# Two passes instead of three for the value products of both attentions, with a join of half tiles

## The reference, cut to what matters

```python
# layer 0: 16 heads of 32; layer 1: 32 query heads of 64 in 8 groups, keys and queries rotated
w = softmax(q @ k.T / sqrt(hd) + causal_mask)
z = w @ v
x = x + z_of_all_heads @ Wo.T          # layer 1: @ w_out.T
```

## Time and profile before

| | us |
|---|---|
| median of 3 runs | 1908.64 (1906.13 to 1909.9) |
| the profiled execution | 1907.17 |
| its span | 1905.7 |
| first attention, to the last add into X | 0 to 250.7 |
| second attention, to the last add into X | 929.4 to 1483.0 |
| mean granted clock of TensorE, share of full | 0.986 |

### The profile page before, as it was taken

One profiled execution on the slowest core, in us unless ns is written; L12 is line 12 of the kernel. 1 busy time (PEld: TensorE's weight loads), 2 busy tenths in 40 slices (PEclk: granted clock), 3 DMA queues, 4 the chain that ended last, 5 costly groups with the idle time before them and its releaser, 6 DMA issues. The chain is left out here.

```text
span 1905.7 us, 30804 instructions
## 1 busy us (share of the span) xinstructions
PE 1805.5 (95%) x10161; PEld 1565.8 (82%) x10167; DVE 1113.3 (58%) x2769; ACT 807.4 (42%) x2063; POOL 1010.0 (53%) x965
## 2 busy tenths in 40 slices
PE   7999989999999999999888999999999999999996
PEld 5888858788999999899667888888888888867795
DVE  6676785763333333335766666666666757566345
ACT  3767633222222222221256566666665433543231
POOL 3444341397883957895457456456453203116783
PEclk9999999999999999999999999999999999999998
DMA  3556430236653645554343234233331210012666
GB/s 116 173 155 205 144 138 0 78 145 226 231 199 126 214 144 180 191 153 127 90 112 95 68 92 117 57 89 93 84 78 56 74 50 1 24 50 84 213 214 195
DMA packets 104551, 232.54 MB, mean 122 GB/s; under 512 B 20672, under 2 KB 20928, under 8 KB 101328
## 3 DMA queue, kind: packets, MB, share of 16 engines
q1 hardware_dynamic: 84080, 144.31, 25.0%
q0 software_dynamic: 19744, 85.47, 13.6%
q10 hardware_dynamic: 576, 0.79, 0.2%
HBM read 126.23 MB, written 57.93 MB: 97 GB/s over the span
## 5 line engine op out<-in xcount | busy, mean ns | idle before, releaser
L712 POOL TENSOR_SCALAR a_E<-a_E,a_inv 128x128 f32<-128x128 f32 (+3 forms) x384 | 213.9, 575 | 237.7 <-DVE a_inv L848 237.7
L745 ACT ACTIVATE a_E<-a_E,a_top 128x512 f32<-128x512 f32 (+3 forms) x384 | 211.1, 565 | 6.0 <-DVE a_top L842 5.9
L153 PE MATMUL bank<-f_UH,f_XH 128*128 x596 | 200.5, 336 | 8.4 <-POOL f_UL L165 3.4
L153 PE MATMUL bank<-f_UL,f_XH 128*128 x596 | 193.2, 324 | 0.0
L153 PE MATMUL bank<-f_UH,f_XL 128*128 x596 | 193.2, 324 | 0.0
L842 DVE CUSTOM_DVE_ANT_0 a_E<-a_causal,bank 128x512 f32<-128x512 bf16 (+3 forms) x384 | 163.6, 480 | 43.0 <-PE bank L1023 31.5
L153 PE MATMUL bank<-a_PHL,a_VH 128*128 128x512 f32 (+3 forms) x768 | 181.1, 325 | 0.9 <-issue 0.6
L737 ACT ACTIVATE a_PHL<-bank 128x512 fp32r<-128x512 f32 (+1 forms) x288 | 131.0, 528 | 112.6 <-PE bank L1039 112.5
L1821 ACT ACTIVATE f_HH<-bank 128x256 fp32r<-128x256 f32 x220 | 59.8, 323 | 232.2 <-PE bank L2218 232.1
L165 DVE TENSOR_TENSOR a_PHL<-bank,a_PHL 128x512 fp32r<-128x512 f32 (+1 forms) x288 | 153.2, 585 | 5.1 <-ACT a_PHL L737 4.8
L1876 DVE TENSOR_TENSOR f_gate<-bank,f_gate 128x352 f32<-128x352 f32 x79 | 41.3, 522 | 192.1 <-PE bank L153 192.0
(11 more groups left out here) (407 smaller groups left out, 4864.8 us busy)
## 6 DMA issues: line engine op xcount, KB each, us to landing
f_uraw<-f_up POOLq DMA_DIRECT2D x18, 1408.0 KB, 6.7
f_xb<-table SPq DMA_DIRECT2D x86, 256.0 KB, 3.2
table<-f_ob SPq DMA_DIRECT2D x86, 256.0 KB, 2.7
table<-a_zeros SPq DMA_DIRECT2D x31, 512.0 KB, 4.3
f_draw<-f_down POOLq DMA_DIRECT2D x27, 512.0 KB, 4.5
a_g<-a_f SPq DMA_DIRECT2D x160, 64.0 KB, 2.0
a_raw<-a_qkv SPq DMA_DIRECT2D x36, 256.0 KB
f_uraw<-f_up POOLq DMA_DIRECT2D x9, 704.0 KB, 4.4
```

The lines of the kernel that those rows point to most:

```text
L153: m = pe.matmul(out, a, b, start=first and i == 0 and j == 0, stop=last and i == n - 1 and j == 2, skip_group_check=not check)
L712: e.tensor_scalar(self.E[sl][:, a], self.E[sl][:, a], self.inv[:, sl, i:i + 1], 0.0, ALU.mult, ALU.add).then_inc(*self.s_nrm.up(N, m - 1, i))
L745: x = e.activation(E, E, ACT.Exp, scale=-1.0, bias=self.top[:, sl, i:i + 1], accum_out=self.total[:, sl, i:i + 1])
```

## The change

- Values: `VH` and `VL` become one tile `V`. A head's high part stands at its own columns, its low part 64 columns further (modulo 128). `_pe_values` multiplies `V` by the high and by the low part of the weights: two passes, 8 products a job in place of 12. The rows of one half of the bank then hold the main part of the heads of that half, the rows of the other half the part of the low values. So a bank is finished and emptied after each half of the 128 rows: after every job in the second attention, after every second one in the first (`opens`, `closes`).
- Emptying: ACT copies its own half into QH (rounded) and the other half into `S`; DVE, now one loop later and behind the reciprocal, writes the rest of its own half into `R`; POOL adds R and S into QL once a pair, ahead of the normalisation, and signals `s_rest`, on which the output products wait.
- The value projection gets a buffer of its own, `W`.
- First attention: output products stand in fours at n = 3 and 7, behind the turning of the values, where they stood in twos; the rounding of the output weights moves.
- Second attention: DVE rotates at the end of its loop; ACT's rounding, DVE's low part and SP's spreading of the rotated tile come one loop later, ACT's at the start of its loop.
- Last step of both: 10 products that only keep PE busy stand before the last four output products.
- The last job but one of the second attention gets a bank of its own; its zeroing of V falls away, and the first attention's is halved.

```diff
-        self.VH, self.VL = sb("VH", [heads, NT, P], F32R), sb("VL", [heads, NT, P], F32R)
+        self.V = sb("V", [heads, NT, P], F32R)
+        self.S, self.R, self.W = sb("S", [T]), sb("R", [T]), sb("W", [T])
...
-            self.FILL = [[("P", K, 1), ("O", 0, -1), ("O", 1, -1)], [("P", 0, 1), ("O", 2, -1), ("O", 3, -1)],
-                         [("P", V, 1)], [("T", 1)], [("P", K, 0, 1), ("O", 4, -1), ("O", 5, -1)],
-                         [("P", 0, 0, 1), ("O", 6, -1), ("O", 7, -1)], [("P", V, 0, 1)], [("T", 0, 1)]]
-            self.SPLIT = {2: (K, 1), 3: (0, 1), 5: (V, 1), 6: (self.wt, 0)}
+            self.FILL = [[("P", K, 1)], [("P", 0, 1)], [("P", V, 1)],
+                         [("T", 1)] + [("O", g, -1) for g in range(TT)],
+                         [("P", K, 0, 1)], [("P", 0, 0, 1)], [("P", V, 0, 1)],
+                         [("T", 0, 1)] + [("O", g, -1) for g in range(TT, NT)]]
+            self.SPLIT = {0: (self.wt, -1), 2: (K, 1), 3: (0, 1), 5: (V, 1)}
...
+    def values_bank(self, m):
+
+        return self.last_bank if m == self.M - 2 and self.opens(self.jobs[m][3]) and self.closes(self.jobs[m][3]) else self.OB
...
@@ def sp
-            if self.rotary is None or m < 1:
-                self._moves(m if self.rotary is None else m - 2)
+            for x in self.projected(m - 2 if self.rotary is not None else m):
+                e.wait_ge(*self.s_lo.after(N, *x))
+                self._move(e, x, 0)
+                if x not in self.shared_moves:
+                    self._move(e, x, 1)
             if self.rotary is not None:
                 for x in self.projected(m):
                     self._turn(x)
-                if m >= 0:
-                    self._moves(m - 1)
...
@@ def pool
-        for z in (self.VH, self.VL):
-            e.memset(z[:, :, :, :].bitcast(F32), 0.0)
+        if 2 * self.hd < P:
+            e.memset(self.V[:, :, :, :].bitcast(F32), 0.0)
...
+            if 4 <= m < self.M + 4 and self.jobs[m - 4][3] == self.heads - 1:
+                j, b, r, h = self.jobs[m - 4]
+                e.wait_ge(*self.s_olo.after(N, j, r, b, self.half(h)))
+                e.tensor_tensor(self.QL[:, r, b * T:b * T + T], self.R[:, :], self.S[:, :], ALU.add).then_inc(
+                    *self.s_rest.up(N, j, r, b))
...
@@ def act
+            if self.rotary is not None and m > 0:
+                self._act_rotated(m - 2)
...
-            if 3 <= m < self.M + 3 and self.jobs[m - 3][3] == self.heads - 1:
+            if 3 <= m < self.M + 3 and self.closes(self.jobs[m - 3][3]):
                 j, b, r, h = self.jobs[m - 3]
+                own, other = self.halves(h)
+                bank = self.k.bank[self.values_bank(m - 3)]
                 e.wait_ge(*self.s_av.after(N, m - 3))
-                e.activation(self.QH[:, r, b * T:b * T + T], self.k.bank[self.OB][:, :], ACT.Copy).then_inc(
-                    *self.s_ohi.up(N, j, r, b))
+                if m - 3 >= self.heads:
+                    e.wait_ge(*self.s_rest.after(N, *self.pair(m - 3 - self.heads)))
+                e.activation(self.QH[own, r, b * T:b * T + T], bank[own, :], ACT.Copy)
+                e.activation(self.S[own, :], bank[other, :], ACT.Copy).then_inc(
+                    *self.s_ohi.up(N, j, r, b, self.half(h)))
...
@@ def dve
+            if 4 <= m < self.M + 4 and self.closes(self.jobs[m - 4][3]):
+                self._dve_low_values(m - 4)
             if self.rotary is not None:
-                if m < 1:
-                    self._dve_low_rotated(m - 2)
-                for x in self.projected(m - 1):
+                for x in self.projected(m - 2):
+                    s = self.slot[x]
+                    e.wait_ge(*self.s_rhi.after(N, *x))
+                    low_part(e, self.f[s], self.f[s].bitcast(F32), self.g[s],
+                             scale=self.scale if x[1] < self.qtiles else None).then_inc(*self.s_lo.up(N, *x))
+                for x in self.projected(m - 1) if m < 0 else []:
                     self._dve_rotate(x)
...
             if self.rotary is not None and m >= 0:
-                self._dve_low_rotated(m - 1)
-            if 3 <= m < self.M + 3 and self.jobs[m - 3][3] == self.heads - 1:
...
+                for x in self.projected(m - 1):
+                    self._dve_rotate(x)
...
+    def _dve_low_values(self, m):
+
+
+        e, N, (j, b, r, h) = self.k.dve, self.name, self.jobs[m]
+        (own, other), a, key = self.halves(h), slice(b * T, b * T + T), (N, j, r, b, self.half(h))
+        bank = self.k.bank[self.values_bank(m)]
+        e.wait_ge(*self.s_ohi.after(*key))
+        if m >= self.heads:
+            e.wait_ge(*self.s_rest.after(N, *self.pair(m - self.heads)))
+        low_part(e, self.R[own, :], bank[own, :], self.QH[own, r, a]).then_inc(*self.s_olo.up(*key))
...
@@ def _pe_fill
+                if g == TT and j == self.STEPS - 1:
+                    self.k.warm(10, bk)
                 if g % TT == 0:
-                    e.wait_ge(*self.s_olo.after(N, j, self.queries[-1], g // TT))
+                    e.wait_ge(*self.s_rest.after(N, j, self.queries[-1], g // TT))
...
@@ def _pe_values
-        if h == 0 and self.OB in emptied:
-            e.wait_ge(*emptied[self.OB])
+        bk = self.values_bank(m)
+        if self.opens(h) and bk in emptied:
+            e.wait_ge(*emptied[bk])
...
-                t = product(e, self.k.bank[self.OB][:, sblk * P:T],
-                            [(self.VH[:, h, b * TT + sblk, :], self.VL[:, h, b * TT + sblk, :])],
-                            [(self.PH[m % 2][:, a], self.PL[m % 2][:, a])],
-                            first=h == 0 and sblk == 0, last=h == self.heads - 1 and ci == 2)
+                for x, weights in enumerate((self.PH, self.PL)):
+                    t = e.matmul(self.k.bank[bk][:, sblk * P:T], self.V[:, h, b * TT + sblk, :], weights[m % 2][:, a],
+                                 start=self.opens(h) and sblk == 0 and x == 0, stop=self.closes(h) and ci == 2 and x == 1)
```

More of the change, by code:

```diff
@@ L507, in split @@
             c, ahead = self.SPLIT[n]
[L508 removed]
+            if 0 <= j + ahead < self.STEPS:
                 of.append((j + ahead, c))
@@ L544, in plan @@
         self.slot, self.free, self.fill_bank, self.score_bank = {}, {}, {}, {}
-        freed, ring, self.staged = [[], []], 0, {}
+        freed, turned, ring, self.staged = [[], []], [], 0, {}
         for m in self.loops:
@@ L549, in plan @@
                     self.score_bank[m, ci], ring = ring % self.SR, ring + 1
+            if m == self.M + 1:
+                self.last_bank, ring = ring % self.SR, ring + 1
             for x in self.fill(m):
@@ L595, in plan @@
                 self.s_av.plan((N, m))
+                if self.closes(h):
+                    for s in (self.s_ohi, self.s_olo):
+                        s.plan((N, j, r, b, self.half(h)))
                 if h == self.heads - 1:
-                    self.s_ohi.plan((N, j, r, b))
-                    self.s_olo.plan((N, j, r, b))
+                    self.s_rest.plan((N, j, r, b))
     def moves(self, j, c, b):
@@ L614, in moves, with half, opens, closes @@
                 [(self.KH[up, 1, a], g[dn, :]), (self.KH[dn, 1, a], g[dn, :]), (self.KL[dn, 1, a], f[dn, :])]]
+    def values_bank(self, m):
+        return self.last_bank if m == self.M - 2 and self.opens(self.jobs[m][3]) and self.closes(self.jobs[m][3]) else self.OB
+    def half(self, h):
+        return h * self.hd // self.HALF
+    def opens(self, h):
+        return h * self.hd % self.HALF == 0
+    def closes(self, h):
+        return (h + 1) * self.hd % self.HALF == 0
+    def pair(self, m):
+        j, b, r, h = self.jobs[m]
+        return j, r, b
+    def low_columns(self, cs):
+        at = (cs.start + self.HALF) % P
+        return slice(at, at + self.hd)
+    def halves(self, h):
+        own = slice(self.half(h) * self.HALF, (self.half(h) + 1) * self.HALF)
+        return own, slice((1 - self.half(h)) * self.HALF, (2 - self.half(h)) * self.HALF)
     def out_weights(self, x, r):
@@ L646, in sp @@
                     self.k.fetch_context()
-    def _moves(self, m):
-        e = self.k.sp
-        for x in self.projected(m):
-            e.wait_ge(*self.s_lo.after(self.name, *x))
-            self._move(e, x, 0)
-            if x not in self.shared_moves:
-                self._move(e, x, 1)
     def _move(self, e, x, half):
@@ L747, in act @@
                     x.then_inc(*self.s_ex.up(N, m, ci))
-            if self.rotary is not None and m >= 0:
-                self._act_rotated(m - 1)
             self._act_fill(m)
```

32 lines of the change are left out of this document (10 added, 22 removed).

## The result

The changed kernel takes 1920.79 us (median of 9 runs, 1909.79 to 1924.28), the kernel before on the same chips 1908.5 us (9 runs): ratio 1.0062, 95% interval 1.0047 to 1.0078. It is slower by about 12 us, and the forecast of 1892 us, as well as the range up to 1909, was wrong. The profiled executions differ by 15.2 us. The profiled executions belong to runs of 1922.15 and 1907.17 us. First the page of after and the core's clock; the earlier trace rows is the first line of before. The last line is the transposes' row of before.

The account below looks back on a forecast made before the run. The prediction took PE to bound the kernel, with POOL's chain next in the second attention; 6 us from the first attention plus 17 from the second less 7 for the clock gave 1892 us, own range 1884 to 1902, wider range 1858 to 1909.

Parts of the forecast that it names:

- What bounds the kernel: Whole kernel: PE, busy 95%, sets the time; next in the second attention's runs is POOL's chain, 7.9 us a tile.
- The third pass: Value products: two passes take 1.27 us instead of 1.90, 0.63 less a job, 60.5 us over 96 jobs if all shows.
- First attention: First attention: 6 us saved in sum, with turning loops of 8.9 or 8.35 us waiting for DVE before the last output product.
- Second attention: Second attention: a half step saves 2.3 us, not 5.0, since the run still waits for POOL; 17 us saved in sum.
- The join: POOL, ahead of the normalisation in every second loop: each join in a run costs 1.73 us rather than 1.29.
- The moved rotation: Second attention: removing DVE's waits on POOL, 1.26 us a tile, is no gain by itself; the normalisation stands behind the same product.
- The clock: TensorE: 11 new waits of 2.05 us and more make the clock fall 4 times, costing 7 us.
- The sum: Whole kernel: 6 + 17 - 7 = 16 us off 1907.17, that is 1891.2; median 1892 us.
- (b): Rival: the clock falls at nearly every new wait, 19 us eat most of 23; 1905 us, chance 0.13.
- (c): Rival: the join delays the transposes in 32 loops of the second attention, 1.73 us each, 55 us; 1923 us, chance 0.10.
- (a): Rival: PE stays the bound and the whole pass shows, 60.5 us; 1848 us, or 1863; chance 0.12.
- (d): Rival, second attention: the swap chain is shorter than counted, each us on a run gives 8; 1876 us, chance 0.15.

Follow-up runs that it names:

- fillers: The full change plus useless products on PE inside its new waits in both attentions; 1910.9 us, ratio 1.0020 to the kernel before.
- first_only: The changed attention in the first stage, the old one in the second; 1917.6 us, ratio 1.0052 to the kernel before.
- the third pair: The full change plus a third pair of rotation buffers in the second attention, turned values staged in that ring again; 1891.8 us, ratio 0.9918 to the kernel before.
- no_join: The full change without ScalarE's copy of the other half and POOL's add, low values' part missing from the outputs; 1896.9 us, ratio 0.9937 to the kernel before.
- twos: The full change with the first attention's output products by twos beside the projections, as before; 1906.5 us, ratio 0.9999 to the kernel before.
- three_twos_late: Full change, third rotation buffer pair, first attention's products by twos, next stage's context fetched at loop 24 instead of 20; 1881.4 us, ratio 0.9862 to the kernel before.

## Why the prediction was wrong, step by step

**What bounds the kernel.** PE's 95% was read rightly, and I saw the chain of 7.9 us a tile through POOL's sine product and SP's transfers, longer than PE's 7.0. What failed is the next step: I counted the chain as getting shorter by the change, with the spreading of tile 7 landed at 20.5 us. It got longer.

**The third pass.** Right in its size on PE: 768 products take 141 us, and a projection loop of the first attention lasts 5.75 us, forecast 5.77. Of its 44 us in the second attention the runs with useless products show 22.

**First attention: 9 us later where 6 earlier was forecast.** The mechanism was right: the last of the four output products waits for VectorE's low part of the values, 2.15 us in three of the five turning loops and 3.35 and 3.56 in the two with ScalarE's rounding of weights (2.1 and 2.6 by my count). With the clock kept up (fillers) the turning loops last 9.24 and 8.65 us, forecast 8.9 and 8.35, and jobs 12 to 27 save 2.0 us, forecast 3.3. Three terms failed. The early jobs: from job 4 to job 12 fillers takes 53.6 us against 50.9 before, a loss of 2.8 where I had 1.9 saved, because job 11's loop goes from 4.1 to 10.15 us and loops 8 to 10 give back only 2.9; I had these cancel. The clock: it fell in three of the five loops in after, in all five in first_only, in none of them in fillers. And the start: after reached the scores of job 0 2.6 us late, which other runs of the same code did by 0 to 3 us, so that this is no fixed cost.

**Second attention: 3 to 6 us longer where 17 shorter was forecast.** The term that failed is the cycle of the rotation's buffers. I let tile 9 be evicted 20.5 us after the start of loop 7, when the spreading of tile 7 has landed. In the half step of the rows it is 1172.82 - 1149.34 = 23.5, in the other four of the middle 21.8 to 22.2, each with a wait of 1.9 to 3.1 us; before it was 21.4 to 22.5. The spreading itself landed at 21.7 to 23.4 us in after; before it landed at 20.9 to 21.2 in four of the five and at 22.4 in the fifth. In the one of the rows it could be issued from 18.2 us (1167.56), 1.5 later than my 16.7, because VectorE's low part starts at 17.3 and takes 0.9; it took 2.4 us to issue and landed 2.7 us after its last issue's end (1169.98). I had left 3.8 us for issue and landing, although my own prices (2.52 and about 2) make 4.5: with them the eviction comes at 21.2, where it was before, and the gain of the run is nearly gone on paper.

```profile
1167.56 0.50 SPq L688 DMA_DIRECT2D a_QH<-a_g  x1
...
1169.38 0.60 SPq L688 DMA_DIRECT2D a_QL<-a_g  x1
```

The rest is ScalarE's order, which I didn't follow at all: the late eviction holds up the rounding of the other buffer's tile. So the last sine product started 38.0 us after loop 7, not 32.0 (34.1 to 35.8 in the other four half steps, 33.7 to 35.1 before), with the join and the normalisation behind it:

```profile
1187.31 1.80 POOL L734 TENSOR_TENSOR a_g<-a_g,a_cos_sin 128x512 f32<-128x512 f32 x1 [4.47 <-DMA a_g<-a_f]
1189.07 1.26 POOL L738 TENSOR_TENSOR a_QL<-a_R,a_S 128x512 fp32r<-128x512 f32 x1
```

Loops 7 to 11 took 38.7 us, against 36.0 before and 33.6 in my count (35.5 to 36.4 in the other four half steps, 35.7 to 37.1 before). The waits at n = 12 (2.35 forecast) add up to 1.8 to 2.4 us. With the third pair the last sine product starts at 31.9 to 32.4 us, forecast 32.0, and the half step is 60.8 and 61.05 us where 61.0 was forecast: the rest of the count holds once this term is removed. Only the first run was counted too dear: with three pairs the time from job 0 to the end of the first half step falls from 114.8 to 105.9 us, where I had taken 1 us. It is not the only way to free this chain, since leaving the joining out brings nearly as much with two pairs.

**The join.** Its place was right, its price high for most: of the 14 joins in the runs of the second attention 6 take 1.71 to 1.74 us, as I had for all, and 8 take 1.26 to 1.30. The rule of the Trainium skill on the shared interfaces was therefore used too simply; the last section shows what the rows say. What I had wrong is that ScalarE's wait for the join (2.43 us at n = 11) would not reach PE: the rounding of the rotated tile and the copies of the probabilities stand behind it, and leaving the joining out gave 24 us.

**The moved rotation**, which I called no gain by itself, gave none with two pairs, and 30 us with three.

**The clock.** The price of a stretch fits: fillers has 17 us less of slow stretches in the two attentions (48 instead of 65 us) and is 8 us faster. The number was wrong: 65 us against 20 before (each with the stretch just ahead of the second attention) is 13 stretches of 3.4 us, 22 us, instead of 4 and 7 us. In the second attention they also followed several short waits in a row (0.47, 0.49, 0.23 and 0.34 us at n = 11), which I hadn't counted.

**The sum.** Forecast and profile are 31 us apart (1891.2 and 1922.15; the median's forecast should have read 1892.7, not 1892): 15 by the clock, some 10 by the second attention's waits (its forecast of 536.6 against 546.2 in after once half of its 27 us of extra slow stretches is taken off), the rest, 5 to 7, by the first one's early jobs and start. **The rivals:** (b) came nearest, with 19 us forecast for the clock and 22 measured, but it kept the gain of 23 whole. (c), the join late in 32 loops, did not happen in that form; its price of 55 us is far from no_join's 24. (a) and (d) lay on the wrong side. The buffers' cycle getting longer by the change was no rival of mine; the chain of 7.9 us a tile was where to look for it.

## What to carry to other kernels

Where a kernel has two buffers for a chain of several engines and transfers, write down the whole cycle of one buffer, with the queue order of each engine that serves both, before you count a gain on the bounding engine; if the cycle is near that engine's time, shorten the cycle or add a buffer first. Add up the landing of each transfer from your own prices; here 0.7 us left out of one sum hid that nothing was gained. Work taken off the bounding engine turned into waits here, and most waits of some 2 us in dense work were followed by a slow clock. To learn what a cut is worth by itself, put useless work of its size back: here it was half. Parts of a change are not to be judged alone: the same move of work was worth 0 with two buffers and 30 us with three, and the join's best place changed sign.

## What the runs showed of the hardware

Nine kernels have output products by fours and no fillers, each with three waits of 2.02 to 2.16 us among dense products in the first attention. In 21 of these 27 cases TensorE's clock fell to 1.2 GHz within 1.4 us of the wait's end, for 3.4 us in 20 of them and 6.8 in one; in 6 it stayed up (jobs 23 and 27 of after are two). Filled with 2.12 us of useless products such a wait was followed by no fall.

Transfers of 64 KB behind two of 1 MB on the same queue took 3.7 to 8.5 us from issue to landing (twos), and 2.0 to 3.0 us with the two moved away (three_twos_late).

When VectorE's and POOL's products of two tiles of the rotation run beside each other, either may pay. At n = 8 of after POOL takes 1.80 us and VectorE 0.69, at n = 10 POOL 1.29 and VectorE 1.52 (timelines of VectorE and POOL, each pair in order):

```profile
1161.42 0.69 DVE L935 TENSOR_TENSOR a_f<-a_f,a_cos_sin 128x512 f32<-128x512 f32 x1 [0.32 <-DMA a_g<-a_f]
...
1177.73 1.52 DVE L935 TENSOR_TENSOR a_f<-a_f,a_cos_sin 128x512 f32<-128x512 f32 x1
```
```profile
1161.47 1.80 POOL L734 TENSOR_TENSOR a_g<-a_g,a_cos_sin 128x512 f32<-128x512 f32 x1 [3.55 <-DMA a_g<-a_f]
...
1177.41 1.29 POOL L734 TENSOR_TENSOR a_g<-a_g,a_cos_sin 128x512 f32<-128x512 f32 x1 [3.31 <-DMA a_g<-a_f]
```

The one that starts second pays, in nearly all pairs of after. VectorE starts 0.04 to 0.05 us ahead in 12: POOL takes 1.76 to 1.80 us and VectorE 0.69. POOL starts 0.3 to 0.7 us ahead in 10: POOL takes 1.27 to 1.30 and VectorE 1.13 to 1.55. In the two where POOL is ahead by less than 0.1 us POOL pays (1.88 and 1.91). The Trainium skill, GPSIMD Engine Reference, section 8, tells of the contention; the rows agree that there is one, and show that its price may fall on VectorE, where the prediction had put all of it on POOL.
